# The front of the state-space units reordered, and unread products on TensorE in its gaps

## What is computed

```python
hidden = _rmsnorm(residual, norm_w)
x, z = jnp.split(hidden @ W_in, 2, axis=-1)            # W_in 128 x 512, D_INNER = 256
x = jax.nn.silu(conv4(x) + conv_b)                     # 4 taps along time, per channel
x_dbl = x @ W_x                                        # 256 x 96: 64 for dt, 16 for B, 16 for C
dt = jax.nn.softplus(x_dbl[..., :64] @ W_dt + b_dt)    # W_dt 64 x 256
A = -jnp.exp(A_log)                                    # 256 x 16
def step(h, inp):
    x_t, dt_t, B_t, C_t = inp
    h = jnp.exp(dt_t[..., None] * A) * h + (dt_t * x_t)[..., None] * B_t[:, None, :]
    return h, jnp.einsum('bdn,bn->bd', h, C_t)
y = (ys + x * D) * jax.nn.silu(z)
out = residual + y @ W_out
```

## Time and profile before

| | us |
|---|---|
| median of 3 runs | 1333.98 |
| the profiled execution | 1338.44 |
| its span, first to last instruction | 1336.6 |
| PE, DVE, ACT, POOL busy | 1213.2, 907.5, 641.2, 235.3 |
| mean granted TensorE clock | 0.963 |

### The profile page before, as it was taken

The page is one execution under the profiler, slowest core; times in us unless marked ns, Lnnn a source line. Parts: engine busy times, 40 slices in busy tenths (PEclk is TensorE's granted clock), DMA queues, the critical chain, the costliest instruction groups (busy, mean ns, idle before and its releaser), DMA issues.

```text
span 1336.6 us, 16894 instructions
## 1 busy us (share of the span) xinstructions
PE 1213.2 (91%) x5959; PEld 787.5 (59%) x6008; DVE 907.5 (68%) x1754; ACT 641.2 (48%) x1183; POOL 235.3 (18%) x201
## 2 busy tenths in 40 slices
PE   5998778999899889899999969789998996989998
PEld 2676444567666455556667744346775664546665
DVE  6755867455567698987665667564455667989765
ACT  3544354543422587952234325454443227969322
POOL 3000100000020074651000010000000102928210
PEclk9999999999999889799999999899999996979999
DMA  6203220000101121220200032200001101212220
GB/s 227 56 32 81 54 75 19 2 1 1 64 1 64 42 79 35 97 85 0 72 24 0 24 88 62 54 3 1 1 1 64 49 16 58 78 58 79 64 72 9
DMA packets 33284, 63.19 MB, mean 47 GB/s; under 512 B 4368, under 2 KB 20016, under 8 KB 33008
## 3 DMA queue, kind: packets, MB, share of 16 engines
q1 hardware_dynamic: 33200, 62.11, 14.9%
HBM read 54.16 MB, written 8.45 MB: 47 GB/s over the span
## 4 chain that ended last, share of the span: by engine, by line
PE 70%; DVE 12%; ACT 9%; DMA 3%; issue 2%; POOL 2%; SPq 2%; another core or an unknown queue 0%; DVEq 0%; ACTq 0%; POOLq 0%
PE bank L1529 13%; PE bank L1531 12%; PE bank L1530 12%; PE bank L1698 9%; PE bank L1538 5%; ACT n_part L1077 4%; DVE a_mx L1410 3%; PE bank L1848 3%; PE bank L1607 3%; ACT n_da L1069 2%; PE bank L1763 2%; POOL n_hc L830 2%; PE bank L1734 2%; PE bank L1668 2%; DMA a_k<-stack_dram 2%
## 5 line engine op out<-in xcount | busy, mean ns | idle before, releaser
L1254 DVE SCALAR_TENSOR_TENSOR f_hl<-bank,f_hh 128x512 fp32r<-128x512 f32 x192 | 131.8, 689 | 130.5 <-ACT f_hh L904 129.8
L904 ACT ACTIVATE f_hh<-bank 128x512 fp32r<-128x512 f32 x192 | 114.7, 597 | 188.9 <-PE bank L1607 150.7
L966 ACT ACTIVATE m_sl<-bank 128x512 f32<-128x512 f32 x144 | 86.0, 599 | 235.3 <-PE bank L1531 234.9
L830 POOL TENSOR_TENSOR n_hc<-n_h,n_cs 128x512 f32<-128x512 f32 x128 | 159.7, 1276 | 180.3 <-DVE n_h L1500 174.5
L1529 PE MATMUL bank<-xT_h,mw_h 128*128 128x512 f32 x288 | 160.6, 558 | 4.4 <-DVEq L532 2.7
L1500 DVE TENSOR_TENSOR_SCAN n_h<-n_da,bank 128x512 f32<-128x512 f32 x128 | 149.7, 1207 | 9.8 <-PE bank L1538 7.3
L1698 PE MATMUL bank<-m_h,mw 128*128 128x512 f32 x288 | 145.6, 594 | 0.0
L1321 DVE TENSOR_TENSOR m_t<-m_sl,bank 128x512 f32<-128x512 f32 x128 | 87.9, 687 | 78.6 <-PE bank L1531 77.5
L1848 PE MATMUL bank<-n_hc,ident 128*128 128x512 f32 x256 | 135.4, 616 | 0.2
L1410 DVE TENSOR_REDUCE a_mx<-bank 128x1 f32<-128x384 f32 (+3 forms) x176 | 105.9, 637 | 42.2 <-PE bank L1804 39.9
L983 ACT ACTIVATE a_p<-bank 128x1024 f32<-128x1024 f32 (+3 forms) x128 | 87.9, 703 | 87.3 <-PE bank L1739 50.9
(11 more groups left out here) (243 smaller groups left out, 2306.3 us busy)
## 6 DMA issues: line engine op xcount, KB each, us to landing
n_cs<-c_dram SPq DMA_DIRECT2D x32, 512.0 KB, 3.7
m_c<-comb_dram SPq DMA_DIRECT2D x28, 512.0 KB, 5.1
stage_fw<-in_fw_dram SPq DMA_DIRECT2D x6, 512.0 KB, 7.1
stack_dram<-R SPq DMA_DIRECT2D x16, 192.0 KB, 2.8
w_stage<-in_mw_dram SPq DMA_DIRECT2D x9, 256.0 KB, 2.7
stack_dram<-R SPq DMA_DIRECT2D x16, 128.0 KB, 2.6
a_q<-stack_dram SPq DMA_DIRECT2D x4, 512.0 KB, 5.1
a_k<-stack_dram SPq DMA_DIRECT2D x8, 256.0 KB, 4.8
```

Source lines behind the costliest of these rows:

```text
L830: n_hcs.by(nc.gpsimd.tensor_tensor(n_hc[:, i % 4, :], n_h[:, i % 4, :], n_cs[:, j % C_RING, i // 2 % 2, :], ALU.mult))
L1254: f_lo.by(V.scalar_tensor_tensor(f_h[1][:, i % 4, :], bank[:, i % 3, :], 0.0, f_h[0][:, i % 4, :].bitcast(F32), ALU.max, ALU.subtract))
```

## The change

A weight `wxd` is made once, in the first unit: PE multiplies the transposed dt part of `W_x` by `W_dt`, ACT copies the result to SBUF. In each state-space unit dt then comes from `n_xc` by `wxd`, four products, and `wx` is used only for the rows of B and C, behind them. In slot 1 the last two gathers of slot 0 go ahead of these. The exponential is taken for each half, ACT copies `n_bT`, `n_ln` lies in PSUM, DVE's steps are done by half, and POOL makes the first half of `n_dtx`. At the end of slot 0's loop the last turn goes ahead of both projections. PE runs 16, 3 and 7 products of 384 columns into bank 6, which nothing reads, ahead of, between and behind the transposes of `n_dtx`.

```diff
         wx = sb("wx", [P, NHALF, 96])
-        wdt = sb("wdt", [64, NHALF, P])
+        wxd = sb("wxd", [P, NHALF, NHALF * P])
         wout = sb("wout", [P, NHALF, P])
...
         stage_rw = spare[:, 0:96 + EXPERTS]
+        wdt, wxT = (spare[0:64, n * NHALF * P:(n + 1) * NHALF * P] for n in (4, 5))
         MW1 = 4 * P
...
         n_brow = n_cs[:, 2, 0, :]
-        n_dtr, n_crow, n_db = n_hc[0:64, 0, :], n_hc[:, 1, :], n_hc[:, 2:4, :]
-        n_abs, n_u, n_ln, n_sq = n_h[:, 0:2], n_h[:, 2:4], n_da[:, 0:2], n_da[:, 2:4]
+        n_crow, n_db = n_hc[:, 1, :], n_hc[:, 2:4, :]
+        n_abs, n_u, n_ln, n_sq = n_h[:, 0:2], n_h[:, 2:4], bank[:, 2:4], n_da[:, 2:4]
...
             tree_weights(0, 1)
+            load(wdt, A["wdt"], wdt_in)
+            load(wxT, A["wxT"], wdt_in)
             batch(1)
...
                     tree_weights(t, which)
-            small = [(t[:], name) for t, name in ((owT, "owT"), (wx, "wx"), (wdt, "wdt"), (wout, "wout"),
+            small = [(t[:], name) for t, name in ((owT, "owT"), (wx, "wx"), (wout, "wout"),
                                                   (amat, "a_log"), (gate_b, "gate_b"), (tri, "tri"),
...
                         n_fill.by(nc.gpsimd.memset(n_xp[:, :, 0:3], 0.0))
-                    else:
+
+                    pool.wait_ge(n_dts.sem, n_dts.at(k, 0))
+                    n_dtx0.by(nc.gpsimd.tensor_tensor(n_dtx[:, 0], n_dt[:, 0], n_xc[p][:, 0], ALU.mult))
+                    if p == 1:
...
                         head_job(kth[u - 1], job, n)
+                    if u == 0 and i == 3:
+
+                        act.wait_ge(w_xd.sem, w_xd.at(0, 0))
+                        w_xds.by(act.activation(flat(wxd[:]), bank[:, 7, :], ACT.Copy))
                     if k == 0 and i in TREE_SPLIT_AT:
...
                 act.activation(preload, half[:, 0, 0:NT], ACT.Exp)
-                act.wait_ge(n_xdb.sem, n_xdb.at(k, 0))
-                n_dtc.by(act.activation(n_dtr, bank[0:64, 4, :], ACT.Copy))
                 for m in range(2):
...
                     n_abss.by(act.activation(n_abs[:, m, :], bank[:, m, :], ACT.Abs, bias=b_dt[:, m:m + 1]))
-                act.wait_ge(n_abss.sem, n_abss.at(k, 1))
-                n_us.by(act.activation(n_u, n_abs, ACT.Exp, scale=-1.0))
-                act.wait_ge(n_us.sem, n_us.at(k, 0))
+                    act.wait_ge(n_abss.sem, n_abss.at(k, m))
+                    n_us.by(act.activation(n_u[:, m], n_abs[:, m], ACT.Exp, scale=-1.0))
                 for m in range(2):
+                    act.wait_ge(n_us.sem, n_us.at(k, m))
+                    if p == 1:
+                        act.wait_ge(n_y.sem, n_y.at(k - 1, m))
                     n_lns.by(act.activation(n_ln[:, m], n_u[:, m], ACT.Ln, bias=1.0))
                     n_sqs.by(act.activation(n_sq[:, m], n_u[:, m], ACT.Square, scale=HALF_ROOT))
+                act.wait_ge(n_btp.sem, n_btp.at(k, 0))
+                n_bts.by(act.activation(flat(n_bT[:]), bank[:, 5, 0:NT * NSTATE], ACT.Copy))
                 for i in range(2):
...
-                dve.wait_ge(n_xdb.sem, n_xdb.at(k, 0))
-                n_crs.by(V.tensor_copy(n_crow[64:96], bank[64:96, 4, :]))
                 if p == 1:
...
                     n_poss.by(V.tensor_scalar(n_pos[p][:, m], bank[:, m, :], b_dt[:, m:m + 1], 0.0, ALU.add, ALU.max))
-                dve.wait_ge(n_btp.sem, n_btp.at(k, 0))
-                n_bts.by(V.tensor_copy(flat(n_bT[:]), bank[:, 5, 0:NT * NSTATE]))
-
-                dve.wait_ge(n_us.sem, n_us.at(k, 0))
-                dve.wait_ge(n_poss.sem, n_poss.at(k, 1))
-                step(V.tensor_scalar(n_cor[p], n_u, 1.0, -1.0, ALU.add, ALU.add))
-                step(V.tensor_tensor(n_pos[p], n_pos[p], n_u, ALU.add))
+                    if m == 1:
+                        dve.wait_ge(n_xdb.sem, n_xdb.at(k, 0))
+                        n_crs.by(V.tensor_copy(n_crow[64:96], bank[64:96, 4, :]))
+                    dve.wait_ge(n_us.sem, n_us.at(k, m))
+                    dve.wait_ge(n_poss.sem, n_poss.at(k, m))
+                    V.tensor_scalar(n_cor[p][:, m], n_u[:, m], 1.0, -1.0, ALU.add, ALU.add)
+                    step(V.tensor_tensor(n_pos[p][:, m], n_pos[p][:, m], n_u[:, m], ALU.add))
                 dve.wait_ge(n_sil.sem, n_sil.at(k, 3))
...
                     dve.wait_ge(n_lns.sem, n_lns.at(k, m))
-                    step(V.tensor_tensor(n_cor[p][:, m], n_ln[:, m], n_cor[p][:, m], ALU.subtract))
+                    step(V.tensor_tensor(n_ln[:, m], n_ln[:, m], n_cor[p][:, m], ALU.subtract))
                     dve.wait_ge(n_sqs.sem, n_sqs.at(k, m))
-                    step(V.scalar_tensor_tensor(n_cor[p][:, m], n_sq[:, m], -1.0, n_cor[p][:, m], ALU.mult, ALU.max))
-                    n_dts.by(V.scalar_tensor_tensor(n_dt[:, m], n_cor[p][:, m], 0.0, n_pos[p][:, m], ALU.min, ALU.add))
-                    dve.wait_ge(n_dts.sem, n_dts.at(k, m))
-                    n_dtxs.by(V.tensor_tensor(n_dtx[:, m], n_dt[:, m], n_xc[p][:, m], ALU.mult))
+                    step(V.scalar_tensor_tensor(n_ln[:, m], n_sq[:, m], -1.0, n_ln[:, m], ALU.mult, ALU.max))
+                    n_dts.by(V.scalar_tensor_tensor(n_dt[:, m], n_ln[:, m], 0.0, n_pos[p][:, m], ALU.min, ALU.add))
+                dve.wait_ge(n_dts.sem, n_dts.at(k, 1))
+                n_dtx1.by(V.tensor_tensor(n_dtx[:, 1], n_dt[:, 1], n_xc[p][:, 1], ALU.mult))
                 dve.wait_ge(n_b0.sem, n_b0.at(k, 0))
                 for m in range(2):
-                    dve.wait_ge(n_dtxs.sem, n_dtxs.at(k, m))
+                    dve.wait_ge((n_dtx0, n_dtx1)[m].sem, (n_dtx0, n_dtx1)[m].at(k, 0))
                     n_db0.by(V.tensor_tensor(drive(m), n_dtx[:, m], n_brow, ALU.mult))
...
                                         [f_h[c][:, i2 % 4, :] for c in range(2)], start=False, stop=m == M1 - 1))
+                    if u == 0 and i == 2:
+
+                        pe.wait_ge(wdt_in, 32)
+                        for m in range(NHALF):
+                            ins = mm(bank[:, 7, m * NHALF * P:(m + 1) * NHALF * P], wxT[:, m * P:(m + 1) * P], wdt,
+                                     start=True, stop=True)
+                        w_xd.by(ins)
+                    if u == 0 and i == 4:
+
+                        pe.wait_ge(w_xds.sem, w_xds.at(0, 0))
                     if after_heads(u) and i < 3:
...
                 n_cvp.by(ins)
+
+            def keep_busy(count):
+
+                for _ in range(count):
+                    mm(bank[:, 6, 0:3 * P], identb, flat(cbf[:]), start=True, stop=True)
...
                     pe.wait_ge(m_res.sem, m_res.at(kth[u - 1], 0))
-                for m in range(2):
-                    pe.wait_ge(n_sil.sem, n_sil.at(k, 2 - p + m))
-                    ins = mm(bank[0:96, 4, :], wx[:, m, :], n_xc[p][:, m, :], start=m == 0, stop=m == 1)
-                n_xdb.by(ins)
                 if p == 1:
...
                     gather(k - 1, last)
-                pe.wait_ge(n_dtc.sem, n_dtc.at(k, 0))
+                for half in range(NHALF):
+                    for m in range(2):
+                        if half == 0:
+                            pe.wait_ge(n_sil.sem, n_sil.at(k, 2 - p + m))
+                        ins = mm(bank[:, half, :], wxd[:, m, half * P:(half + 1) * P], n_xc[p][:, m, :],
+                                 start=m == 0, stop=m == 1)
+                    n_dtp.by(ins)
                 for m in range(2):
-                    n_dtp.by(mm(bank[:, m, :], wdt[:, m, :], n_dtr, start=True, stop=True))
+                    ins = mm(bank[64:96, 4, :], wx[:, m, 64:96], n_xc[p][:, m, :], start=m == 0, stop=m == 1)
+                n_xdb.by(ins)
                 for c in range(NT):
...
                     out_of_states(k - 1, 0)
+                pe.wait_ge(n_sil.sem, n_sil.at(k, 3))
+                keep_busy(16)
                 pe.wait_ge(n_bts.sem, n_bts.at(k, 0))
...
                 for m in range(NHALF):
-                    pe.wait_ge(n_dtxs.sem, n_dtxs.at(k, m))
+                    if m == 1:
+                        keep_busy(3)
+                    pe.wait_ge((n_dtx0, n_dtx1)[m].sem, (n_dtx0, n_dtx1)[m].at(k, 0))
                     ins = rows(lambda t: dtx_rows(t)[:, m * P:(m + 1) * P],
...
                 n_dxt.by(ins)
+                keep_busy(7)
                 pe.wait_ge(n_poss.sem, n_poss.at(k, 1))
...
                 for i in range(2, last + 1):
-                    back_to_scan(k, p, i)
-                    if p == 0 and i >= last - 1:
-                        if i == last - 1:
-                            ready(u + 1)
-                        project(k + 1, 1, i + 1 - last)
+                    if p == 1 or i < last:
+                        back_to_scan(k, p, i)
+                    if p == 0 and i == last - 1:
+                        back_to_scan(k, p, last)
+                        ready(u + 1)
+                        project(k + 1, 1, 0)
+                        project(k + 1, 1, 1)
                     if i >= 4:
...
```

(3 more changed lines are left out.)

11 lines of the change are left out of this document (7 added, 4 removed).

## The result

The changed kernel took 1326.55 us (median of 6 runs, 1324.17 to 1328.11) beside 1333.45 for the kernel before on the same chip: ratio 0.9947, 95% interval 0.9934 to 0.996, 6.9 us faster. The forecast was 1324.7, 9.3 us faster.

A forecast was written before the change was run, and what follows sets the result against it. PE has most of the chain, but the four state-space units were priced as a front chain over all engines plus an ACT-paced loop: 2 x (3.6 + 1.5) - 0.9 = 9.3 off 1333.98 gives 1324.7 us, range 1321 to 1333.5.

The forecast's parts named there:

- The front of slot 0: Small operations before slot 0's loop: shorter chain puts n_dtx 1 3.25 us earlier, ACT's loop start 3.7; 3.6 taken per slot.
- Scan 0: First scan on DVE in a state-space unit: 3.1 us earlier in slot 0, 1.6 earlier in slot 1.
- rival (c): First B row arrives late by DMA in each unit, moving the first scan by 1.1 us: 1329 us, chance 0.10.
- the loop is ACT's: State-space loop: ACT, busy 41.2 of 41.6 us, paces it, so front gains or losses pass to the unit's end.
- Slot 1: Second state-space unit of each pair: PE bounds its front, unread products take 0.7 us; gain 1.4 to 1.6, 1.5 taken.
- The dummies' pitch: Unread products on PE: spaced 0.18 us at full clock, 0.32 at half; 0.28 and 0.42 with uncovered weight loads.
- What the dummies do: Unread products around n_dtx's transposes: full clock worth 0.45 us there, at most 0.3 later in the loop, not counted.
- The order of the last turns: End of slot 0's loop: new order of last projections counted as nothing, bounds 0 and 0.6 us.
- The first unit: Making the folded weight there: two 256-column products on PE's chain cost 0.9 us.
- Rival (a): Unread products run at half clock and stand in the way, 9.4 + 0.9 us slower: 1344.3 us, chance 0.13.
- (b): Clock falls in some slots and comes back; gain 2.4 us in slot 0, -0.5 in slot 1: 1331 us, chance 0.13.
- (d): Front's gain given back because DVE or POOL, not ACT, holds both loops: 1333 us, chance 0.07.

The follow-up runs named there:

- e7: Changed kernel with the write of the B and C rows held until n_dt 0 is there; 1336.72 us, ratio 1.0013 to the kernel before.
- e4: Changed kernel with 32 unread products instead of 16 ahead of the first transposes of n_dtx; 1333.08 us, ratio 0.9989 to the kernel before.
- e9: Changed kernel with the first half of n_dtx back on DVE instead of POOL; 1329.1 us, ratio 0.9948 to the kernel before.
- e1: Changed kernel without the 26 unread products of each unit; 1327.98 us, ratio 0.995 to the kernel before.
- e3: Changed kernel with the end of slot 0's loop as before, last two turns and two projections alternating; 1324.9 us, ratio 0.9926 to the kernel before.
- e10: Changed kernel with dt again by way of n_dtr, the first unit's two products kept but unread; 1333.64 us, ratio 0.9991 to the kernel before.
- e8: Changed kernel with each of the 26 unread products replaced by an f32 transpose of the identity; 1327.21 us, ratio 0.9943 to the kernel before.

## Why the prediction was right

Step by step, by the prediction's own numbers:

- **The front of slot 0.** Abs 0 1.8 earlier: 1.78. n_dtx 1 3.25: 3.26. L1093 3.7: 3.72. These match so well because forecast and check both start from the long form, with the 16-column products at half clock. Over the six slots 0 of before L1093 gained 3.2, and the slot 3.3 for the forecast 3.6.
- **Scan 0** of slot 0 was to be 3.1 earlier. It was 3.25 in the second pair and 2.4 in the first, where the B row is late, as in rival (c). The margin was to be 0.4; it was -0.78 in the first pair, -0.04 in the second, and the row was in time in slot 1. My chain took 1.6 from the write to the request of the row, which held in three of four units; in the first the request left 2.5 behind the write, beside the transfer of q8. I had looked for the danger in the C rows queued behind and not in a transfer that the kernel doesn't issue. The price that (c) put on a late row was wrong for slot 0, where 1.2 of it is free, and right for slot 1 (e7).
- **That the loop is ACT's** held: e4 and e9 pass their delays on. It needed the second bound, scan 0 + 41.9, which I did not have. ACT's loop became 0.3 shorter where the clock stayed up, the bound I gave.
- **Slot 1.** 1.5 forecast, 1.7 measured. The collision is there, but costs 0.37 at the transposes and nothing at the end, since scan 0 (1.64 earlier, forecast 1.6) holds this loop. I had charged this slot to ACT's L1077 and a collision, so the number is near for a partly wrong reason.
- **The dummies' pitch.** I took 0.18 and no less; 0.163 was measured, outside my bounds at the full clock. At half clock 0.32, as scaled.
- **What the dummies do.** I credited them with the 0.45 at the transposes of slot 0: e1 says 2.3 over the four units, of which 0.6 is a late B row; the 1.7 that are left are nearly twice my 0.9, and all in slot 0.
- **The order of the last turns** at nothing: e3.
- **The first unit.** 0.9 forecast. The two products stand on the chain for 1.06; the mean of ten profiles with them is 68.6 (67.9 to 69.8), of four without 68.0 (67.1 to 68.7), so the scatter leaves the 0.6 between them open.
- **Rival (a)** did not come, as the clock stayed at 1.00 up to the transposes; e10 shows it where PE idles between the dummies and what they are for. **Rivals (b) and (d)** did not come either: no front of the change fell to half clock, and e4 and e9 pass a delay on to the end.

The sum: forecast 10.2 - 0.9 = 9.3; the stretches gave 10.0 and the first unit took 0.6 back, 9.4; the pooled medians 8.8. That the sum is this close is in part luck: each slot 0 gained 0.3 less than forecast and each slot 1 0.2 more, and the first unit took 0.3 less. Singly undone, the parts are worth 6.9 (fold), 3.1 (POOL), 2.3 (dummies) and about 0 (order), together 12.3 for 10.0: they overlap. Some 1.2 of this is that without the fold the dummies get in the way (e10), and 0.6 is the late row of e1. What the halves and the copy of `n_bT` on ACT give alone was not tried, nor was the fold alone in the kernel before, so how the 10.0 divide among the parts stays open.

## What to carry to other kernels

A loop has a start bound for each engine that can pace it, so write down all of them with their slack (here 1.2 us for the scan in slot 0, none in slot 1) before pricing a late transfer. Work that only keeps the clock up is worth what TensorE has on the path behind it, 1.7 us over two slots 0 here and nothing in slot 1, where a scan sets the loop. Put it so that no long gap follows it: behind a gap of 3.61 the next three dummies ran at half clock and stood in the way (e10). When a transfer is late, look at the queues that the kernel doesn't issue on as well. Anchor on milestones and compare stretch by stretch over several profiles: two profiles differed by 14 us, the change by 9.

## What the runs showed that I had not expected

- Filler transposes, 0.11 apart, kept the granted clock at 1.00 in three of four fronts (e8), though a stage with 1.97 of 4 us of transposes had stayed at half in the earlier trace rows.
- 65 to 75 us at half clock in the state-space stretches of before, 0 to 7 in after: e1 lies between, at 41, and from there to after the clock was worth only 1.7 us.
- A 64 KB write to DRAM takes 1.6 us, and 2.0 to 2.6 when a 16 KB transfer of the instruction queue starts with it (8 of 56 writes).
- The same 16-column products of before took 3.12 in one execution and 1.96 in another. One kernel's runs spread over 9 us (1329.7 to 1338.8).
